# Four chained layers on one core: x in two loads, a weight load three places later, a product over 128 rows

## What is computed

```
x = x + L0(x)   expert = argmax(cond_8): silu(x Wup + bup) * (x Wgate + bgate), times Wdown, + bdown; hidden 256
x = x + L1(x)   x W_base^T + b + 2 * sum over e of cond_8[b,e] * Bs[e] As[e] x     (rank 16, 8 experts)
x = x + L2(x)   x times (sum over g of cond_8[b,g] * weight[g] * mask)^T + bias
x = x + L3(x)   shared gelu MLP (hidden 512) + the best 2 of 8 experts of the softmax of cond_8, weighted
```

## Time and profile before

| | |
|---|---|
| median of 3 runs | 150.93 us (150.54 to 151.47) |
| profiled execution | 151.12 us, of which the span from first to last instruction is 149.2 us |
| PE matmul, weight loads | 145.5 us (98%), 136.0 us (91%) |
| DVE, ACT, POOL | 108.3 us (73%), 71.5 us (48%), 93.5 us (63%) |
| mean granted TensorE clock | 1.000 |

### The profile page before, as it was taken

One profiled execution on the slowest core, in us unless ns is written; L12 is line 12 of the kernel. 1 busy time (PEld: TensorE's weight loads), 2 busy tenths in 40 slices (PEclk: granted clock), 3 DMA queues, 4 the chain that ended last, 5 costly groups with the idle time before them and its releaser, 6 DMA issues.

```text
span 149.2 us, 3185 instructions
## 1 busy us (share of the span) xinstructions
PE 145.5 (98%) x1102; PEld 136.0 (91%) x1102; DVE 108.3 (73%) x226; ACT 71.5 (48%) x140; POOL 93.5 (63%) x109
## 2 busy tenths in 40 slices
PE   7999999999999999999999999999999999999992
PEld 3889999999978899999989999999999999999891
DVE  2935576668996577787876877877688896858792
ACT  3776445560465645454444535445445434346560
POOL 1169999999200395977977577968587999500000
PEclk9999999999999999999999999999999999999999
DMA  3999999986345675497195088637047606000052
GB/s 65 419 404 397 403 412 396 422 336 217 135 153 169 177 181 179 134 340 247 60 290 206 3 282 275 221 100 321 0 105 321 209 2 211 7 0 0 4 211 70
DMA packets 13919, 30.15 MB, mean 202 GB/s; under 512 B 1360, under 2 KB 8016, under 8 KB 13776
## 3 DMA queue, kind: packets, MB, share of 16 engines
q1 hardware_dynamic: 13472, 28.76, 54.6%
q10 hardware_dynamic: 432, 1.19, 2.3%
HBM read 24.70 MB, written 1.05 MB: 173 GB/s over the span
## 4 chain that ended last, share of the span: by engine, by line
PE 97%; DVE 1%; issue 0%
PE pair L603 23%; PE pair L593 15%; PE acc L652 11%; PE pair L534 10%; PE pair L610 10%; PE acc L637 7%; PE acc L542 5%; PE acc L661 5%; PE pair L498 2%; PE pair L579 2%; PE pair L554 2%; PE acc L489 2%; PE acc L524 1%; PE pair L524 1%; PE acc L498 1%; DVE lora_raw L843 1%
## 5 line engine op out<-in xcount | busy, mean ns | idle before, releaser
L810 DVE TENSOR_TENSOR hid_lo<-hid,hid_hi 128x512 fp32r<-128x512 f32 (+1 forms) x42 | 37.7, 898 | 17.0 <-ACT hid_hi L465 16.4
L400 POOL TENSOR_TENSOR duo_lo<-raw_duo,duo_hi 128x512 fp32r<-128x512 f32 x36 | 47.9, 1331 | 2.9
L465 ACT ACTIVATE hid_hi<-hid 128x512 fp32r<-128x512 f32 (+1 forms) x42 | 25.7, 611 | 43.4 <-DVE hid L817 39.2
L397 POOL CAST duo_hi<-raw_duo 128x512 fp32r<-128x512 f32 x36 | 27.5, 764 | 25.2 <-PE pair L603 19.3
L817 DVE TENSOR_TENSOR hid<-pair,act 128x512 f32<-128x512 f32 (+1 forms) x50 | 32.9, 662 | 4.6 <-PE pair L603 4.1
L603 PE MATMUL pair<-x_duo,duo_hi 128*128 128x256 f32 x192 | 35.2, 282 | 0.0
L450 ACT ACTIVATE act<-pair 128x512 f32<-128x512 f32 x47 | 27.6, 588 | 9.3 <-PE pair L603 7.0
L603 PEld LDWEIGHTS pair<-x_duo,duo_hi 128*128 128x128 f32 x192 | 29.7, 188 | 0.4
L603 PE MATMUL pair<-x_duo,duo_lo 128*128 128x256 f32 x96 | 27.0, 281 | 0.0
L593 PE MATMUL pair<-x_hl,shared_hi 128*128 128x512 f32 x64 | 20.5, 401 | 0.0
L603 PEld LDWEIGHTS pair<-x_duo,duo_lo 128*128 128x128 f32 x96 | 18.1, 189 | 0.0
(11 more groups left out here) (101 smaller groups left out, 202.6 us busy)
## 6 DMA issues: line engine op xcount, KB each, us to landing
raw_duo<-experts SPq DMA_DIRECT2D x12, 768.0 KB, 5.6
ring<-experts SPq DMA_DIRECT2D x16, 386.5 KB, 7.4
raw_solo<-experts SPq DMA_DIRECT2D x8, 768.0 KB, 4.3
x_duo<-x_hl SPq DMA_DIRECT2D x24, 128.0 KB, 3.3
x<-xT ACTq DMA_DIRECT2D x1, 1024.0 KB, 6.3
lora_raw<-x SPq DMA_DIRECT2D x4, 256.0 KB, 2.7
raw_solo<-shared SPq DMA_DIRECT2D x1, 768.0 KB, 10.9
out<-lora_raw SPq DMA_DIRECT2D x3, 256.0 KB, 2.6
```

The costliest lines, as they stand in the source:

```text
L397: pool.tensor_copy(duo_hi[:, j % HALVES, piece(n)], raw_duo[:, j % RAWS, piece(n)])\
L400: pool.tensor_tensor(duo_lo[:, j % HALVES, piece(n)], raw_duo[:, j % RAWS, piece(n)], duo_hi[:, j % HALVES, piece(n)].bitcast(F32), ALU.su ...
L465: act.activation(hid_hi[:, k % SPLITS, half(u, i)], hid3[:, u % PAIRS, half(u, i)], ACT.Copy)\
L810: dve.tensor_tensor(hid_lo[:, k % SPLITS, half(u, i)], hid3[:, u % PAIRS, half(u, i)], hid_hi[:, k % SPLITS, half(u, i)].bitcast(F32), ALU ...
```

## The change

Three edits. x is loaded in two halves of 512 KB: batches 0 to 7 still on ACT's queue, batches 8 to 15 on SP's queue behind the first four expert loads, with a semaphore each; PE and DVE wait for the second at batch 8. The first duo's load, with the wait for the sort ahead of it, stands behind expert load 13 and not behind load 11. `ones` and `payload_sum` get 128 rows, the 112 new rows of `payload_sum` are set to zero by POOL at the start, and L566 (L571 after) runs over 128 rows.

```diff
-        ones = sb("ones", [B, P])
+        ones = sb("ones", [P, P])
...
-        payload_sum = sb("payload_sum", [B, 3, SLOTS])
+        payload_sum = sb("payload_sum", [P, 3, SLOTS])
...
-        x_in, shared_in = sem("x_in"), sem("shared_in")
+        x_in, shared_in = [sem("x_in0"), sem("x_in1")], sem("shared_in")
...
             for b in range(4):
                 load0(b)
+            sp.dma_start(x[:, B // 2 * P:], xT[:, B // 2 * P:]).then_inc(x_in[1], 16)
             expert0 += values(mybir.EngineType.SP, at_row[0:1, 4:B], E)
...
-            for b in range(SLOTS0, SLOTS0 + 2):
+            for b in range(SLOTS0, B - 2):
                 load0(b)
             sp.wait_ge(slots_done, 1)
             duo_expert = values(mybir.EngineType.SP, slot_row[0:1, SLOTS:SLOTS + 2 * DUOS], E)
             load_duo(0)
-            for b in range(SLOTS0 + 2, B):
+            for b in range(B - 2, B):
                 load0(b)
...
             pool.memset(ones[:, :], 1.0).then_inc(ones_set, 1)
+            pool.memset(payload_sum[:, :, :], 0.0).then_inc(sum_set, 1)
...
-            pool.tensor_tensor(payload_sum[:, :, :], payload[:, :, 0, :], payload[:, :, 1, :], ALU.add)\
+            pool.wait_ge(sum_set, 1)
+            pool.tensor_tensor(payload_sum[0:B, :, :], payload[:, :, 0, :], payload[:, :, 1, :], ALU.add)\
                 .then_inc(payload_done, 1)
...
-            act.dma_start(x[:, :], xT).then_inc(x_in, 16)
+            act.dma_start(x[:, 0:B // 2 * P], xT[:, 0:B // 2 * P]).then_inc(x_in[0], 16)
...
                 pe.wait_ge(e0_in[b % SLOTS0], 16 * (b // SLOTS0 + 1))
+                if b == B // 2:
+                    pe.wait_ge(x_in[1], 16)
...
-            pe.wait_ge(x_in, 16)
+            pe.wait_ge(x_in[0], 16)
...
-            dve.wait_ge(x_in, 16)
+            dve.wait_ge(x_in[0], 16)
...
+                if b == B // 2:
+                    dve.wait_ge(x_in[1], 16)
                 dve.wait_ge(down0_done, b + 1)
```

More of the change, by code:

```diff
@@ L213, in build_kernel @@
         route, weigh = sem("route"), sem("weigh")
-        ones_set, zeros_set = sem("ones_set"), sem("zeros_set")
+        ones_set, zeros_set, sum_set = sem("ones_set"), sem("zeros_set"), sem("sum_set")
         exp_done = sem("exp_done")
```

## The result

Slower. Over 20 runs each, the changed kernel took 151.84 us (151.24 to 153.20) and the kernel before 150.56 (150.20 to 151.51); the ratio is 1.0068, 95% interval 1.0052 to 1.0084. The forecast was 150.6 and its range ended at 151.6. The rival that ended on this side, POOL's late start, had 151.6.

What follows compares the result with a forecast made beforehand. PE, busy 98% of the span, was taken as the bound. Terms -0.37 + 0 + 0 + 0.04 = -0.33 us, from the 150.93 us median, gave 150.6 us, range 149.9 to 151.6.

Steps and rivals of the forecast that it cites:

- POOL's late start: Slower rival: first duo lands at 28.4 us, POOL ends at 39.9, 1.0 us reaches PE; 151.6 us, chance 0.12.
- The product over 128 rows: L566, the sort's last product on PE: both gaps around it go, its cost falls from 0.59 to 0.22, gaining 0.37 us.
- the row count costs nothing: Rival at L566: the gaps have another cause, such as bank change or semaphore, so no gain; 150.9 us, chance 0.13.
- x in halves: Loads of x and experts: experts 0 to 3 land 1.3 us sooner, later ones unchanged; counted as nothing, within 0.1 us.
- The duo's move: First duo lands near 27.4 us, POOL ends near 38.9, its lock holds DVE's L783; 0.04 us reaches PE at 44.26.
- The base: Profiled execution 151.12 us, median 150.93 taken as base; margins there: batch 12's weights 0.5 us, first expert 1.5 us.
- the experts begin sooner: Faster rival: PE's expert start hangs on x or first weights, up to 1.3 us more gain; 149.3 us, chance 0.03.

## Why the prediction was wrong

**The product over 128 rows: right.** 0.37 us forecast, 0.36 in the profile, 0.24% in the time alone. Both gaps went, as by the Trainium skill's "TensorEngine Tiling (Array Packing)", Key Properties, by which a change of the tiling mode drains TensorE. The rival that the row count costs nothing falls. That the median time agrees so well is in part luck, since the fastest runs gained only 0.08 us.

**x in halves: the step that failed.** It said "From expert 4 on the same bytes have gone before, so all lands as it did" and "I count the edit as nothing, within 0.1 us". Bytes were counted and a rate was assumed. The shared weights landed 1.13 us late in the changed kernel and 1.50 late with this edit alone, which costs 0.88%, 1.3 us. Part is the 4 KB pieces 8 KB apart (packed halves: 0.21%, not clear of no change), part a slow spell of the experts' packets, whose cause stays open. The other half of the step held: x and the first experts did land sooner (the first expert at 8.12), and nobody waited for them.

**The duo's move: the lock right, its size and its path wrong.** "That is 0.04 us" became 0.92. It was worked out as POOL's end plus 0.55, and both ends moved. The duo landed at 28.5 because the stream of loads was late, and with that "a full expert load later than I think", as the rival had it with 28.4 and 151.6 us. And PE was sooner than the profile had it. Without the halves the duo landed at 27.24 and POOL ended at 38.77, as forecast (27.4 and 38.9), and DVE was still held by 0.87, since it came at 37.77 and not at 38.76. The path was another too. That "the 0.04 goes through to PE" was read from PE's wait at 44.26 for `hid_lo`, but that wait is 0.29 us in both kernels. PE takes DVE's low part itself, at its first shared piece, 0.12 us behind its end (39.81 and 39.94 before, 40.61 and 40.72 now), so it had no slack there at all.

**The base.** All margins were taken from one execution in which PE's preparation was late. For batch 12, "they had 0.5 us of margin" was true of it, and gone in others. A margin smaller than the scatter of the start is none. The same holds for the 1.5 us that it gave the first expert: with x whole and PE early (the product and the duo's move, with POOL held), that expert landed at 9.92 and PE began at 10.03, after a wait of 0.40.

**The rivals.** POOL's late start is shown, with chance 0.12 given to it; that its 151.6 lies near the measured 151.84 is part luck, since PE's two waits in the L0 loop weren't in it. Its condition was put down to the order of issues, where the sum looked firm; the link from the halves to the landing of the duo was not drawn. That the experts begin sooner with x in halves didn't show: PE was early by 0.86 us through its own preparation, and with x whole it began at 9.77 to 9.87 as well. In an execution like the one with the wait of 0.40 the edit could have gained that much; no run isolates it.

## What to carry to other kernels

Splitting a load isn't free though the bytes are the same: look at the step between its pieces in DRAM, and check GB/s, not the DMA share. Moving a load behind others moves all that its consumer does next to the work of another engine that may exclude it, as POOL did DVE here; add up where that consumer ends and what starts there, for the earliest PE and not for one profile. When two instructions of 1 us start within 0.1 us of each other on two engines that exclude one another, their order is part of the schedule: where POOL came first, PE lost 1.0 us. Whether a wait that fixes the order pays is not clear here: it narrowed the spread of one kernel and gained nothing in another.

## What the runs showed of the hardware

- From 11 to 13 us, pieces of 4 KB at a step of 8 KB moved at 298 to 333 GB/s beside the experts' 3,092-byte ones, at a step of 12 KB at 401 and packed at 400 to 411, with the DMA share at 0.96 to 1.01 in all. A piece took 204 to 220 ns on the mean in four profiles at 8 KB, and 159 to 169 in four at 12 KB or packed.
- In the slow spell from 8 to 10 us the changed kernel's 3,092-byte packets took 164 ns on the mean, before 122; the median is 122 in both, so a few slow ones make it, up to 0.96 us long.
- A two-operand subtraction of DVE that begins inside POOL's ends 0.54 to 0.55 us behind POOL's end, in the changed kernel and its relatives as before. Where DVE begins first, even by 0.02 us (52.38 against 52.40 in the changed kernel), its own takes 0.69 and POOL's 1.8 instead of 1.3.
- The step of the preparation's fp32 products (256 columns) changes from 0.427 to 0.216 us, a half as between 1.2 and 2.4 GHz, after 0 to 5 of them, by execution, in the same kernel too (five and three in the two profiles of the kernel before). The trace's record of the granted clock begins with that step, at the full 2.4 GHz: at 6.19 and 5.49 us in those two, at 4.46 in the changed kernel. For the time ahead of it there is no record, and the 1.00 that a view prints there is no reading. PE had been at work since 0.8 us. It moves the start of all that follows by up to 1.1 us.
